# Local attention: scores as tiles of 64 rows by 64 queries, queries copied as they are

## The reference

```
# x: (4 sequences of 512 tokens, 128); 16 heads of 64; window 32
q, k, v = split(x @ Wqkv);  q, k = l2norm(q)*qs, l2norm(k)*ks, rotated (scale and 1/scale)
sim  = (q . k) * 8          # a query sees itself and the 32 tokens before it
sim  = where(mask, -max, sim)
out  = softmax(sim) @ v @ Wo
x    = x + out              # then shift, layer norm, gated feed-forward
```

## Time and profile before

| | us |
|---|---|
| median of 3 runs | 5544.11 (5533.84 to 5544.77) |
| the profiled execution | 5523.66 |
| its span | 5521.9 |
| first L795 and last L784 of the six layers | at 235.9 and 2588.3 |
| PE busy | 4022.7 (73%) |
| DVE busy | 3786.7 (69%) |
| ACT busy | 2632.8 (48%) |
| POOL busy | 2173.7 (39%) |

### The profile page before, as it was taken

One profiled execution on the slowest core, in us unless ns is written; L12 is line 12 of the kernel. 1 busy time (PEld: TensorE's weight loads), 2 busy tenths in 40 slices (PEclk: granted clock), 3 DMA queues, 4 the chain that ended last, 5 costly groups with the idle time before them and its releaser, 6 DMA issues. The chain is left out here.

```text
span 5521.9 us, 77266 instructions
## 1 busy us (share of the span) xinstructions
PE 4022.7 (73%) x25236; PEld 2563.8 (46%) x25236; DVE 3786.7 (69%) x7355; ACT 2632.8 (48%) x6895; POOL 2173.7 (39%) x1599
## 2 busy tenths in 40 slices
PE   4399698698698798798868759666666665876666
PEld 2166366366366466466343433333333333544443
DVE  5698498497597597597263653799999998322323
ACT  2188388388387487486222211333333333353433
POOL 0276276276275375374121200366666665000000
PEclk7699799899899899899677779655555555677777
DMA  0011011011011011111000000000000000000000
GB/s 16 28 43 42 29 40 43 30 41 43 29 42 40 32 42 37 35 42 35 10 1 9 1 23 0 1 1 1 1 1 1 1 1 1 7 13 5 5 5 8
DMA packets 47608, 108.18 MB, mean 20 GB/s; under 512 B 8832, under 2 KB 8960, under 8 KB 45696
## 3 DMA queue, kind: packets, MB, share of 16 engines
q1 hardware_dynamic: 47232, 103.41, 6.2%
HBM read 29.98 MB, written 1.05 MB: 6 GB/s over the span
## 5 line engine op out<-in xcount | busy, mean ns | idle before, releaser
L873 POOL TENSOR_TENSOR slabs<-slabs 128x512 f32<-128x512 f32 x768 | 975.9, 1299 | 522.8 <-DVE slabs L807 522.8
L1639 DVE MAX8 slabs<-slabs 128x8 f32<-128x512 f32 x1084 | 691.6, 679 | 58.0 <-ACT slabs L1576 58.0
L606 PE MATMUL psum<-slabs 128*128 128x512 f32 x768 | 407.8, 657 | 272.1 <-DVE slabs L807 160.1
L1665 POOL TENSOR_SCALAR slabs<-slabs 128x512 f32<-128x512 f32 x256 | 399.7, 1561 | 471.6 <-DVE slabs L1645 471.6
L749 ACT ACTIVATE slabs<-slabs 128x96 f32<-128x96 f32 x1536 | 551.7, 360 | 42.6 <-PE psum L650 42.4
L1560 ACT ACTIVATE slabs<-slabs 128x512 f32<-128x512 f32 x316 | 211.8, 720 | 728.2 <-DVE slabs L1645 728.2
L862 POOL TENSOR_TENSOR slabs<-slabs 128x768 f32<-128x768 f32 x192 | 344.9, 1796 | 535.3 <-DVE slabs L784 534.7
L1498 PE MATMUL psum<-constants,slabs 128*128 128x128 f32 x1264 | 301.9, 402 | 301.0 <-POOL slabs L1668 300.0
L1641 DVE MATCH_REPLACE8 slabs<-slabs 128x512 f32<-128x512 f32 x768 | 513.0, 675 | 0.0
L1489 PE MATMUL psum<-slabs 8*128 8x512 f32 (+1 forms) x632 | 346.6, 1089 | 164.3 <-ACT slabs L1576 164.2
L642 PEld LDWEIGHTS psum<-weights,slabs 128*128 128x128 f32 x3072 | 372.2, 192 | 100.6 <-issue 86.1
(11 more groups left out here) (358 smaller groups left out, 8508.3 us busy)
## 6 DMA issues: line engine op xcount, KB each, us to landing
slabs<-slabs SPq DMA_DIRECT2D x192, 192.0 KB, 2.5
slabs<-slabs SPq DMA_DIRECT2D x192, 128.0 KB, 2.5
slabs<-F SPq DMA_DIRECT2D x6, 2756.5 KB, 10.3
slabs<-slabs SPq DMA_DIRECT2D x144, 64.0 KB, 2.1
weights<-S SPq DMA_DIRECT2D x4, 645.0 KB, 3.8
weights<-M SPq DMA_DIRECT2D x1, 2184.0 KB, 9.1
weights<-R SPq DMA_DIRECT2D x2, 1079.5 KB, 5.1
slabs<-x SPq DMA_DIRECT2D x1, 1024.0 KB, 4.9
```

Of the source, the lines that this page charges most:

```text
L606: last = nc.tensor.matmul(ps[:, i, :], tokens, w(name, 512 * half, 512), start=True, stop=True)
L873: nc.gpsimd.tensor_tensor(out[:, at, :], normed[:, at, :], table, ALU.mult).then_inc(rope_done, 1)
L1639: nc.vector.max(eight, work[side] if k else scores[slot + side]).then_inc(picked[b], 1)
L1665: nc.gpsimd.tensor_scalar(kept[n % 2], scores[slot], tops[:, slot, TOPK - 1:TOPK], None, ALU.is_ge).then_inc(kept_ready, 1)
```

## The change

The block-diagonal operand goes. The queries are copied as the transposes leave them, 128 partitions by 512 columns in one ACT instruction. The scores are 16 matmuls (32 instructions in a profile), each 64 rows (one head) by 64 columns (one window's queries) against 96 keys. Four following ones take the four quarters of the array: rows by head, columns by window. The two heads of a pair go to two PSUM banks (4 and 5), the two windows to partitions 0 to 63 and 64 to 127. So a partition is now a query of the tile, and the 8 blocks of 96 scores are the 8 heads, where before they were pairs and windows; the first-tile mask becomes one mask over 128 partitions and one DVE instruction instead of two. `weigh` reads its probabilities from other columns of the same buffer, with the same shapes. The zeroing of `qBD` goes.

```
-    qBD = m.slab(7)[:, 256:1280].rearrange("p (n w h q) -> p n w h q", n=PAIRS, w=2, h=2)
+    qT = m.slab(7)[:, 256:768].rearrange("p (n q) -> p n q", n=PAIRS)
...
-            nc.gpsimd.memset(m.slab(7)[:, 256:1280], 0.0)
...
-                pe.wait_ge(qT_copied, 2 * u + 2)
+                pe.wait_ge(qT_copied, u + 1)
...
                 for n in range(GROUPED):
-                    c, k = n // 2, n % 2
-                    keys = kT[:, PAIRS * half + c, t * P + k * WINDOW:t * P + k * WINDOW + KEYS]
-                    last = nc.tensor.matmul(SCORES[:, n // 4, n % 4, :], qBD[:, c, k, :, :], keys, start=True, stop=True)
+                    c, h = n // 2, n % 2
+                    for k in range(2):
+                        keys = kT[64 * h:64 * h + 64, PAIRS * half + c, t * P + k * WINDOW:t * P + k * WINDOW + KEYS]
+                        queries = qT[64 * h:64 * h + 64, c, k * WINDOW:k * WINDOW + WINDOW]
+                        last = nc.tensor.matmul(ps[k * WINDOW:k * WINDOW + WINDOW, 4 + h, KEYS * c:KEYS * c + KEYS], queries, keys,
+                                                start=True, stop=True)
...
-                for h in range(2):
-                    rows = slice(64 * h, 64 * h + 64)
-                    nc.scalar.activation(qBD[rows, :, :, h, :], QT[rows, :, :, :], ACT.Copy).then_inc(qT_copied, 1)
+                nc.scalar.activation(qT, QT, ACT.Copy).then_inc(qT_copied, 1)
...
-                if t == 0:
-                    for k in range(2):
-                        ...
+                shape = mask[1 if t else 0].rearrange("p (o r j) -> p o r j", o=1, r=1).broadcast_to([P, 2, 4, KEYS])
+                last = nc.vector.tensor_tensor(masked.rearrange("p (b n) j -> p b n j", b=2), SCORES, shape, ALU.add)
```

More of the change, by code:

```diff
@@ L524, in _ @@
                                         scale, ALU.mult)
-        windowed_attention(nc, m, w, tables, shifted, qBD, hA, hB)
+        windowed_attention(nc, m, w, tables, shifted, qT, hA, hB)
         shift_tokens(nc, hB, m.slab(12))
@@ L533, in _, with windowed_attention @@
             nc.scalar.activation(g_out.rearrange("p (b t) -> p b t", b=BATCH), hA[:, :, 1:PADSEQ], ACT.Silu)
-def windowed_attention(nc, m, w, tables, shifted, qBD, hA, hB):
+def windowed_attention(nc, m, w, tables, shifted, qT, hA, hB):
     ps = m.psum
@@ L544, in windowed_attention @@
     roped = m.slab(14)[:, 0:1024].rearrange("p (h d) -> p h d", d=HD1)
-    turned = m.slab(14)[:, 1024:2048].rearrange("p (n k q) -> p n k q", n=PAIRS, k=2)
+    turned = m.slab(14)[:, 1024:2048].rearrange("p (n q) -> p n q", n=GROUPED)
     masked = m.slab(15)[:, 0:GROUPED * KEYS].rearrange("p (n k) -> p n k", n=GROUPED)
@@ L558, in windowed_attention @@
     QK = ps[:, 0:2, :].rearrange("p b (h d) -> p (b h) d", d=HD1)
-    QT = ps[:, 6, :].rearrange("p (n k q) -> p n k q", n=PAIRS, k=2)
+    QT = ps[:, 6, :].rearrange("p (n q) -> p n q", n=PAIRS)
     KT = ps[:, 6, :].rearrange("p (n t) -> p n t", n=PAIRS)
     SCORES = ps[:, 4:6, 0:4 * KEYS].rearrange("p b (n k) -> p b n k", n=4)
-    PT = ps[0:KEYS, 7, :].rearrange("p (n k q) -> p n k q", n=2, k=2)
+    PT = ps[0:KEYS, 7, :].rearrange("p (n q) -> p n q", n=4)
     V, CT, OUT = ps[:, 2, :], ps[:, 3, :], ps[:, 2, 0:P]
@@ L662, in weigh @@
                         last = nc.tensor.matmul(ps[rows, 3, WINDOW * n:WINDOW * n + WINDOW], v[u % 4][:, k, c * P + 64 * h:c * P + 64 * h + 64],
-                                                turned[0:KEYS, c, k, rows], start=True, stop=True)
+                                                turned[0:KEYS, PAIRS * h + c, k * WINDOW:k * WINDOW + WINDOW], start=True, stop=True)
                 last.then_inc(pv_product, 1)
@@ L741, in copy_probs @@
                     act.wait_ge(pv_product, u)
-                nc.scalar.activation(turned[0:KEYS, 2 * part:2 * part + 2, :, :], PT, ACT.Copy).then_inc(pT_copied, 1)
+                nc.scalar.activation(turned[0:KEYS, 4 * part:4 * part + 4, :], PT, ACT.Copy).then_inc(pT_copied, 1)
             def exponential(u):
@@ L822, in mask_scores @@
                     dve.wait_ge(exp_done, u)
-                src = ps[:, 4:6, 0:4 * KEYS].rearrange("p b (n k j) -> p b n k j", n=2, k=2)
-                if t == 0:
-                    for k in range(2):
[L826 to L831, removed]
+                shape = mask[1 if t else 0].rearrange("p (o r j) -> p o r j", o=1, r=1).broadcast_to([P, 2, 4, KEYS])
+                last = nc.vector.tensor_tensor(masked.rearrange("p (b n) j -> p b n j", b=2), SCORES, shape, ALU.add)
                 last.then_inc(masked_step, 1)
@@ L2141, in window_masks @@
     seen = (q <= k) & (k <= q + REACH)
-    return np.concatenate([np.where(s, 0, MASKED) for s in (seen & (k >= REACH), seen)], 1).astype(np.float32)
+    first = np.arange(P)[:, None] >= WINDOW
+    return np.concatenate([np.where(s, 0, MASKED) for s in (seen & ((k >= REACH) | first), seen)], 1).astype(np.float32)
 def pad_cols(a, n):
```

## The result

| | before | after |
|---|---|---|
| median | 5544.44 (5533.84 to 5544.85) | 5669.13 (5662.22 to 5678.23) |
| span of the profiled execution | 5521.9 | 5670.9 |
| drops of the granted clock inside the steady parts | 0 | 75 |

After over before is 1.023, with a 95% interval from 1.0216 to 1.0245: 125 us slower. A drop is counted where the record of the granted clock goes from 1.00 to 0.50 after the fill and before the end of a layer's attention; the six layers have 14, 13, 12, 10, 13 and 13.

What follows compares the result with a forecast made beforehand. Bound: a loop of DVE, POOL and the tail of PE's odd iteration. Terms: 0 (scores) + 0 (copies) + 0 (mask) - 1 (zeroing) + 90 (clock) = +89 us on 5544, so 5633 us; range 5534 to 5672.

Steps and rivals of the forecast that it cites:

- Rival 1: In the even iterations' gap the clock holds and all savings become idle time: 5543 us; chance 0.18, and 0.11 more.
- second branch: The clock holds because score tiles go two abreast and the gap stays near 0.2 + 1.2 us; chance 0.11.
- Rival 3: Score tiles on PE don't overlap and take 3.84 us in place of 1.92: 5790 us; chance 0.04.
- rival 2: PE's saving reaches the loop through an earlier second L650, removing 0.29 us waits: 5514 to 5521 us; chance 0.05.
- The number of drops: Clock falls in odd iterations after the even iteration's gap: 10 of 13 possible in each of six layers.
- The price: Cost of one clock fall on PE's dense stretch from L606, taken from the layers' fills: 1.5 us.
- the forecast's own one: Range of the case that the clock falls, from 5 to 13 falls a layer: 5580 to 5670 us.
- The gap that I forecast: PE's idle time around the transposes in the even iteration, between scores and L606: 0.86 + 1.20 = 2.06 us.
- The scores: Score matmuls on PE take 1.1 us a unit instead of 1.92; the saving is off the loop, worth 0.
- The way to the loop: A slow L606 delays the second L650, which releases the exponentials; their wait grows from 0.29 to about 1.8 us.
- The copies: One query copy on ACT instead of two saves 0.6 us a unit, hidden by DVE's lateness: worth 0.
- The masks and the zeroing: One DVE mask instead of two saves 0, at most 7 us; dropping one POOL memset saves 1 us, once.

Runs made afterwards that it cites:

- e3: The kernel before, with every second score matmul left out from each layer's second unit on: 5657.0 us, 1.0209 of the kernel before.
- e9: The changed kernel with its score matmuls reordered so that four in a row use one quarter of the array: 5546.14 us, 1.0007 of the kernel before.
- e5: The changed kernel with four dummy matmuls ahead of the query transposes in even iterations: 5556.2 us, 1.0026 of the kernel before.
- e10: The changed kernel with its score matmuls reordered so that neighbours go to two quarters of the array: 5679.84 us, 1.0238 of the kernel before.
- e1: The changed kernel with the scores of even units issued twice into the same place: 5581.19 us, 1.0063 of the kernel before.
- e4: The changed kernel with the query copy again as two instructions of 64 rows: 5666.51 us, 1.0225 of the kernel before.
- e8: The kernel before, with the output projection moved from the odd iteration to behind the even iteration's scores: 5503.2 us, 0.9925 of the kernel before.
- e7: The changed kernel with the output projection moved behind the even iteration's scores, plus four dummy matmuls in odd iterations: 5518.96 us, 0.9955 of the kernel before.

## Why the prediction was right, and where its numbers were off

**The mechanism holds.** The saved PE time became idle time, the clock fell, and it fell on the dense stretch behind L605. e3 gives the loss without the change, e9 gives the change without the loss, and e5 takes it away by extra work. Rival 1 (the clock holds) is out with 75 drops. Its second branch had the gap stay near 0.2 + 1.2 us with tiles two abreast; in e10, which is that case, they take 1.27 us and not 1.73, leave 0.99 + 1.20 us of idle and cost 72 drops. e9 takes rival 1's time, but because there no gap opens. Rival 3 (no overlap) is out with 0.89 us, and rival 2 (the saving reaches the loop) with the sign of the result.

**The sum, 89 us, measured 125.** Two terms were mis-sized. The number of drops: I took 10 a layer of 13 possible; it was 75 in all, that is 12.5 a layer. The price: I took 1.5 us from the fills; the pair of iterations grew from 9.23 + 9.62 to 10.37 + 10.10, which is 1.62, and 125/75 is 1.66. 75 x 1.62 = 121 us leaves 4. The result is within my range (5534 to 5672), at its upper edge, and just within the forecast's own one.

**Why more drops than I took.** I treated them as separate chances. They don't look it: a pair with a drop in it takes 20.3 to 20.5 us, the next low span starts 20.5 us after the last, and so in each layer the drop meets the same place again for most of the way. The third, fourth and fifth layers show pairs without one (9.30 and 9.56 us in the fourth), after which it comes back; e1 shows whole layers with none next to layers with 11. No run shifts the loop against the drops, so this account is read from the spacings and not tested.

The gap that I forecast as 0.86 + 1.20 = 2.06 us is 0.49 + 2.27 = 2.76. Before and after, DVE and POOL in the even iteration:

```profile
379.62 0.20 DVE L784 RECIPROCAL slabs<-slabs 128x8 f32<-128x8 f32 x1 [0.23 <-ACT slabs L749]
...
385.37 1.83 DVE L815 TENSOR_TENSOR slabs<-slabs 128x512 f32<-128x512 f32 x1
387.12 0.16 DVE L801 TENSOR_TENSOR slabs<-slabs 128x16 f32<-128x16 f32 x1
```

```profile
387.18 0.20 DVE L784 RECIPROCAL slabs<-slabs 128x8 f32<-128x8 f32 x1 [0.85 <-ACT slabs L749]
...
392.91 0.68 DVE L815 TENSOR_TENSOR slabs<-slabs 128x512 f32<-128x512 f32 x1
393.53 1.23 DVE L801 TENSOR_TENSOR slabs<-slabs 128x16 f32<-128x16 f32 x1
```

```profile
389.24 5.48 POOL L866 TENSOR_TENSOR slabs<-slabs 128x512 f32<-128x512 f32 x4
```

L801, on 16 numbers, is over at 394.76 and POOL at 394.72, where L801 takes 0.17 us at 404.95 with POOL idle: again a small instruction held beside POOL's work. In the row of before the one that takes long is L815. That changes how the gap is split and not how long it is: from L815's start to L801's end it is 1.91 us before and 1.85 after. What made the gap longer is PE's side. Its scores are 0.2 us shorter than the 1.1 I took, and they start 0.64 us ahead of L815 (392.27 and 392.91) where they started 0.06 ahead, since DVE's L784 in the iteration waited 0.85 us for the exponentials where it had waited 0.23.

**The scores** took 0.89 us, below the 0.9 to 1.2 that I named and near the bound for four abreast (0.87), not the 1.1 that I took. This had no share in the error of the sum: e10 with 1.27 us lost as much.

**The way to the loop** was right, and the wait by which I wanted to recognise it was not. From L605 over the second L652 and the exponentials to L784 it is 1.69 us longer, and that is the whole loss of the pair. I expected it to show as the exponentials' wait for the second L650, grown from 0.29 to about 1.8 us; that wait is 8.4/12 = 0.70. The slow projection also delays the squares and so DVE's L795 to L807 by 1.5 us, and with them ACT's root, after which only 0.70 is left to wait for PE. I had said that L795 doesn't start on L702; with the slow projection it does. I had also called L650 the only place where PE is on the loop. DVE waited for PE at L790 as well:

```profile
DVE slabs L790 <- PE psum L673: 3.6, 13, 0.3
```

Before the change that wait cost nothing, as L815 behind it was held until POOL had finished.

**Small terms.** The copies are worth 0, shown by e4. The masks and the zeroing weren't tested apart. e3 puts all but the shorter scores at about 12 us, and e9 against the runs of before beside it (3.1 us slower, its interval includes none) shows that together they bring nothing that can be told. The clock in the steady part was 0.92 (I said near 0.95), and a pair at 20.47 us is an iteration of 10.2 (I said 10.1). PE's busy time was to fall by 150 us at equal clock; it went from 4022.7 to 4029.3, at a lower clock, so that sign can't be read.

**The two rules of the Trainium skill.** The Trainium skill, page "TensorE: Matmul & The Clock Gate", section "HAM oscillation — how this bites in real kernels", describes a loop that loses the clock in every round, at a single wait for a DMA between two bursts of matmuls. The trace agrees for 75 of some 78 pairs, though this loop waits in two shorter pieces. The Trainium skill, page "TensorEngine Tiling (Array Packing)", section "Tiling Modes", says that a change of tiling mode drains the engine. Here L643 starts at 392.27 while L630, of the other shape, is put down until 391.31 + 1.02 = 392.33. The profile only models where matmuls end, so this shows that a drain costs no time that can be seen, and not that there is none.

## What to carry to other kernels

Before you shorten the work of an engine that waits anyway, ask what the longer wait does: here 1 us saved per unit on TensorE cost 1.6 us per pair of units, since the granted clock went down at the end of the gap and the projection behind it ran at 1.2 GHz. Look for existing gaps, and for a fill or drain stage in the same trace that shows what a slightly longer one does. If the clock does fall, first move work that is there anyway into the gap (the best version, e8, is the old kernel with one projection moved: 0.9925), or choose an order that keeps the engine busy for longer (e9), and only then add dummy work (e5, e7).

## What I had not expected of the hardware

- Order alone sets how well small tiles overlap: 32 instructions of 64 rows by 64 columns with 96 moving columns took 0.89 us with four quarters in turn, 1.27 with two, and 2.03 when four matmuls in a row used one quarter.
- 64 of them in the first order took 1.55 us (e1), so the second 32 cost 0.66: the other 0.23 of the 0.89 are the start and the end of a burst.
- A drop of the clock can lock to the loop: once begun, it came back every 20.5 us for most of a layer, and the slowed pair of iterations had nearly that length, 20.3 to 20.5 us. Which of the two follows the other wasn't tested.
